# Reordering one time step of two coupled recurrences (a gated recurrent layer and a leaky gated layer) on four engines

## What is computed

```python
# layer 0
z = sigmoid(x_t @ W_z + h @ U_z + cond @ C_z + b_z)
r = sigmoid(x_t @ W_r + h @ U_r + cond @ C_r + b_r)
hh = tanh(x_t @ W + (r * h) @ U + cond @ C + b)
h = (1 - z) * h + z * hh            # x1_t = x_t + h
# layer 1, on x1
gate = sigmoid(h1 @ Wh.T + x1_t @ Wz.T + b)
h1 = tanh(h1 * (1 - alpha) + gate * x1_t)   # x2_t = x1_t + h1
# layers 2 and 3: a scan with forget and input gates, then low-rank adapted dense layers
```

## Time and profile before

| | us |
|---|---|
| median of 3 runs (986.84 to 991.89) | 990.21 |
| the profiled execution | 990.85 |
| its span | 989.0 |
| PE busy | 943.0 (95%) |
| DVE busy | 802.5 (81%) |
| ACT busy | 647.3 (65%) |
| POOL busy | 221.2 (22%) |

### The profile page before, as it was taken

How to read it: one execution, slowest core, us unless ns; L and a number is a source line. 1 busy time by engine, 2 the same in 40 slices (tenths; PEclk the granted TensorE clock), 3 DMA queues, 4 the chain that set the end, 5 groups by cost and what they waited for, 6 DMA issues and landing times.

```text
span 989.0 us, 112546 instructions
## 1 busy us (share of the span) xinstructions
PE 943.0 (95%) x50966; PEld 766.4 (77%) x50966; DVE 802.5 (81%) x2372; ACT 647.3 (65%) x2862; POOL 221.2 (22%) x430
## 2 busy tenths in 40 slices
PE   6699999999999999999999999969999999999996
PEld 5699999999999999999999998335555555555554
DVE  2378778878788778777878787799999999999992
ACT  2478777777777777777777776336455556555552
POOL 0011111111111111111111111324434334434340
PEclk7699999999999999999999999979999999999998
DMA  6113312310010100100101001100011000001001
GB/s 218 41 55 112 110 50 95 111 35 27 24 37 24 37 24 27 34 27 24 37 24 37 24 27 33 28 1 25 24 37 34 24 24 24 24 31 41 24 24 43
DMA packets 38294, 42.01 MB, mean 42 GB/s; under 512 B 5120, under 2 KB 31232, under 8 KB 37120
## 3 DMA queue, kind: packets, MB, share of 16 engines
q1 hardware_dynamic: 36832, 40.55, 13.2%
q10 hardware_dynamic: 1440, 1.18, 0.4%
HBM read 32.80 MB, written 8.91 MB: 42 GB/s over the span
## 4 chain that ended last, share of the span: by engine, by line
PE 57%; DVE 29%; issue 7%; ACT 4%; DMA 1%; ACTq 1%; POOL 0%; DVEq 0%; POOLq 0%
PE bank L788 30%; PE bank L734 22%; DVE arena L667 10%; DVE early L686 4%; DVE early L677 4%; ACT cand_kept L391 2%; DVE early L690 2%; DVE early L684 2%; DVE early L671 2%; DVE early L665 2%; DVE none_h L604 2%; PE bank L906 2%; PE bank L923 1%; DMA bias<-in_bias 1%; PE bank L877 1%
## 5 line engine op out<-in xcount | busy, mean ns | idle before, releaser
L734 PE MATMUL bank<-x_ahead,early 128*32 128x64 f32 x12376 | 345.7, 224 | 5.9 <-ACT bank L358 3.2
L734 PEld LDWEIGHTS bank<-x_ahead,early 128*32 128x32 f32 x12376 | 239.7, 111 | 3.3 <-issue 3.3
L788 PE MATMUL bank<-none_h,early 128*32 128x32 f32 x16384 | 203.1, 199 | 8.8 <-issue 4.9
L280 POOL TENSOR_TENSOR x<-x_f,h_gx 128x64 f32 x256 | 87.6, 342 | 529.4 <-PE bank L788 528.3
L788 PEld LDWEIGHTS bank<-none_h,early 128*32 128x32 f32 x16384 | 180.6, 110 | 27.4 <-DVE none_h L604 13.5
L906 PE MATMUL bank<-x,wl 128*128 (+1 forms) x384 | 182.3, 614 | 0.9 <-DVE rank_rows L646 0.9
L788 PE MATMUL bank<-rh_f,early 128*32 128x32 f32 x8192 | 151.0, 199 | 5.0 <-DVE rh_f L592 2.2
L906 PEld LDWEIGHTS bank<-x,wl 128*128 128x128 f32 x384 | 69.2, 192 | 89.0 <-issue 89.0
L788 PEld LDWEIGHTS bank<-rh_f,early 128*32 128x32 f32 x8192 | 122.1, 112 | 7.0 <-DVE rh_f L592 5.0
L604 DVE TENSOR_TENSOR_SCAN none_h<-zero_z,cand_kept 128x64 f32<-128x64 f32 x512 | 121.6, 279 | 5.3 <-ACT cand_kept L391 3.9
L402 ACT ACTIVATE h_gx<-h_pre 128x64 f32<-128x64 f32 x256 | 68.7, 268 | 81.0 <-DVE h_pre L630 81.0
(11 more groups left out here) (95 smaller groups left out, 1294.4 us busy)
## 6 DMA issues: line engine op xcount, KB each, us to landing
x_in<-in_x SPq DMA_DIRECT2D x34, 256.0 KB, 2.7
x_ahead<-in_x SPq DMA_DIRECT2D x130, 64.0 KB, 1.8
arena<-in_w SPq DMA_DIRECT2D x8, 1024.0 KB, 5.6
out<-y SPq DMA_DIRECT2D x32, 256.0 KB, 2.5
rank_rows<-in_bias_rows SPq DMA_DIRECT2D x1, 1024.0 KB, 5.0
arena<-scratch SPq DMA_DIRECT2D x64, 16.0 KB
early<-in_cx SPq DMA_DIRECT2D x1, 768.0 KB, 4.5
early<-in_wx SPq DMA_DIRECT2D x1, 768.0 KB, 6.3
```

The costliest lines, as they stand in the source:

```text
L280: pool.tensor_tensor(x2[:, :, :, s], x1_f[:, u % LOOP], h1_gx[:, u % 2, :, :, 0], ALU.add).then_inc(x2_done, 1)
L734: mm = pe.matmul(out[32 * j:32 * j + 32], weights(k, j, m), moving(k), start=False, stop=False, tile_position=(0, 32 * j), skip_group_chec ...
L788: mm = pe.matmul(out[32 * j:32 * j + 32], weights(k, j, m), moving(k), start=False, stop=k == 1, tile_position=(0, 32 * j), skip_group_che ...
```

## The change

Instructions of a step are put in another order on PE, ACT and DVE, one is left out, and some waits change. keep_f and its sigmoid go; cand_kept gets (z - 1) h, made by one scalar_tensor_tensor on DVE from zero_z, the tanh is taken of the negated input, and the state scan subtracts instead of adding. On PE both first reset quarters come first, z's mostly behind the reset halves; 32 wide loads, U, layer 1's gate, 32 wide loads follow. "hole" and `late_keep` go. On ACT layer 1's tanh stands behind the reset sigmoids and belongs to one step earlier; its gate comes behind the candidate's tanh, and the reset seeds wait for it. On DVE gate * x1 and the sum of layer 1 come first in a step, x1 of the step before stands behind r * h. r_done and cand_done are counted down by PE, so DVE waits on constants. POOL waits on z_done instead of gate_pre, and its last 16 steps stand behind its loop. SP issues the second x_in load of a turn after the chunk c == 3 of the next one. At the end there is one step of layer 1 more to finish.

```diff
-            def next_turn(n, others=()):
+            def next_turn(n, others=(), first=False):
...
+                    if c == 3 and not first:
+                        next_steps(n - 1, 1)
                     if c == 6:
                         next_steps(n, 0)
...
-                next_steps(n, 1)
@@ POOL
-                    pool.wait_ge(gate_pre, s + LAG + 2)
+                    if last and u >= BODY - LAG - 1:
+                        pool.wait_ge(gate_pre, s + LAG + 2)
+                    else:
+                        pool.wait_ge(z_done, s + LAG + 2)
@@ ACT
-                act.activation(keep_f[:], pre_z[par][:, :, v, :], ACT.Sigmoid, scale=-1.0).then_inc(z_done, 1)
...
-                                   ACT.Tanh).then_inc(cand_done, 1)
+                                   ACT.Tanh, scale=-1.0).then_inc(cand_done, 1)
...
+                    t = n * BODY + u
+                    reset_gate(n, u)
+                    if not first or u > LAG:
+                        second_state(n, u)
+                    elif u:
+                        act.activation(idle[:, u:u + 1], var_eps[:], ACT.Copy).then_inc(h1_done, 1)
+                    update_gate(n, u)
+                    if u % STEPS == 0 and (u or not first):
+                        if first and u <= LAG + 1:
+                            act.wait_ge(gate_pre, u - 1)
+                        else:
+                            act.wait_ge(gate_done, t - LAG - 1)
+                        seed_gate(((u - STEPS) // STEPS) % 2)
+                    candidate(n, u)
+                    if not first or u >= LAG:
                         second_gate(n, u)
...
                     if u % STEPS:
...
+                            act.wait_ge(gate_done, t - LAG + 1)
+                        seed_reset((u // STEPS) % 2, reset_seeded)
                     else:
...
                         seed_keep(1 - (u // STEPS) % 2)
@@ DVE
+            def kept_state(n, u):
+                t, now = n * BODY + u, (u + 1) % 2
+                dve.wait_ge(z_done, t + 1)
+                dve.scalar_tensor_tensor(cand_kept[:, u % 2, :, :, 1], zero_z[:, u % 2, :, :, 1], 1.0,
+                                         none_h[:, now, :, :, 1], ALU.subtract, ALU.mult).then_inc(kept_done, 1)
...
                 for m in range(HALVES):
-                    dve.wait_ge(cand_done, 2 * t + m + 2)
+                    dve.wait_ge(cand_done, m + 1)
                     if m == 0:
-                        dve.wait_ge(kept_done, 2 * t + 2)
+                        dve.wait_ge(kept_done, t + 1)
                     dve.tensor_tensor_scan(pairs(none_h, m), pairs(zero_z, m), pairs(cand_kept, m),
-                                           0.0, ALU.mult, ALU.add).then_inc(h_done, 1)
+                                           0.0, ALU.mult, ALU.subtract).then_inc(h_done, 1)
...
-                    reset_state(n, u)
-                    if second:
+                    if not first or u > LAG:
                         second_gated(n, u)
+                        second_sum(n, u)
+                    reset_state(u)
+                    if u:
+                        first_output(n, u - 1, first)
+                    elif not first:
+                        first_output(n - 1, BODY - 1)
+                    kept_state(n, u)
                     next_state(n, u)
-                    if second:
-                        second_sum(n, u)
-                    first_output(n, u, first)
@@ PE, first_gates
                 pe.wait_ge(h_done, 1)
                 reset(0, 0)
-                keep(0, 0)
-                keep(0, 1)
+                pe.wait_ge(cand_done, 2)
+                reset(0, 1)
+                update(0, 0)
                 pe.wait_ge(h_done, 2)
-                reset(1, 0, taken=h_done).then_inc(r_pre, 1)
-                reset(0, 1)
+                reset(1, 0, taken=(h_done, cand_done)).then_inc(r_pre, 1)
                 reset(1, 1).then_inc(r_pre, 1)
-                keep(1, 0)
-                mm = keep(1, 1)
-                if late_keep:
-                    mm = late_keep()
-                mm.then_inc(z_pre, 1)
+                update(0, 1)
+                update(1, 0)
+                update(1, 1).then_inc(z_pre, 1)
@@ PE, turn
+                for u in range(LOOP):
+                    later = 1 - u // STEPS
+                    first_gates(u)
+                    if u % STEPS == 0:
+                        pe.wait_ge(ahead_loaded[later], 16)
+                        pe.wait_ge(reset_seeded, 2)
+                        ahead_first(later, 0, 0)
+                        ahead_first(later, 0, 1).then_inc(reset_seeded, -2)
+                    else:
+                        ahead_second((u - LAG) % LOOP, later)
+                    first_cand(u)
+                    second_gate(u)
+                    if u % STEPS == 0:
+                        ahead_first(later, 2, 0)
+                        ahead_first(later, 2, 1)
+                    else:
+                        ahead_first(later, 1, 0)
+                        ahead_first(later, 1, 1).then_inc(ahead_loaded[later], -16)
```

More of the change, by code:

```diff
@@ L93, in build_program @@
         rstd = sb("rstd", [P, 1])
-        idle = sb("idle", [P, 2 * LAG])
+        idle = sb("idle", [P, LAG + 1])
         normed = sb("normed", [P, SLAB])
@@ L219, in next_turn @@
                         sp.dma_start(dst, src).then_inc(done, 16)
-                next_steps(n, 1)
-            next_turn(0, [(dst[:], io[name], tail_in) for dst, name in TAIL_LOADS])
+            next_turn(0, [(dst[:], io[name], tail_in) for dst, name in TAIL_LOADS], first=True)
             for w in range(4):
@@ L405, in turn @@
                 for u in range(BODY):
-                    second = not first or u >= LAG
-                    gates_first(n, u)
-                    if second:
+                    t = n * BODY + u
[13 more added lines that the diff above has]
+                    if not first or u >= LAG:
                         second_gate(n, u)
-                    candidate(n, u)
-                    t = n * BODY + u
                     if u % STEPS:
-                        seed_reset((u // STEPS) % 2, 2 * t + 2)
-                    else:
-                        if second or u:
-                            act.wait_ge(z_done, 2 * t)
+                        if first and u < LAG:
+                            act.activation(idle[:, 0:1], var_eps[:], ACT.Copy).then_inc(idle_done, 1)
+                            act.wait_ge(idle_done, 1)
+                        else:
+                            act.wait_ge(gate_done, t - LAG + 1)
+                        seed_reset((u // STEPS) % 2, reset_seeded)
+                    else:
+                        if u or not first:
+                            act.wait_ge(z_done, t)
                         seed_keep(1 - (u // STEPS) % 2)
-                        if second:
[L419 to L426, removed]
                     if first and u == LAG:
@@ L612, in first_output @@
                     dve.wait_ge(x2_done, t - LOOP + 2)
[L613 to L616, removed]
-                    dve.wait_ge(scanned, u + 1)
                 dve.tensor_tensor(x1_f[:, u % LOOP], x_in[:, slot, u % SLOT], none_h[:, nxt, :, :, 1],
@@ L728, in recur, with ahead @@
                 return mm
-            def ahead(out, m, weights, moving, parts=range(HALVES)):
-                for k in parts:
+            def ahead(out, m, weights, moving):
+                for k in range(HALVES):
                     for j in range(SLABS):
@@ L736, in ahead, with ahead_first @@
                 return mm
-            def ahead_first(par, gate, m, parts=range(HALVES)):
+            def ahead_first(par, gate, m):
                 out = (pre_rh[par][m][:, 0], pre_z[par][:, m], pre_rh[par][m][:, 1])[gate]
@@ L772, in _ @@
             pe.wait_ge(seeded, 3)
-            for gate, m in ((0, 0), (0, 1), (2, 0), (2, 1)):
-                ahead_first(0, gate, m)
-            ahead_first(0, 1, 0)
-            ahead_first(0, 1, 1, (0,)).then_inc(ahead_loaded[0], -16)
+            for gate, m in ((0, 0), (0, 1), (1, 0), (1, 1), (2, 0), (2, 1)):
+                mm = ahead_first(0, gate, m)
+            mm.then_inc(ahead_loaded[0], -16)
             pe.wait_ge(hidden_in, 16 * len(HIDDEN_LOADS))
@@ L784, in _, with quarter @@
             pe.wait_ge(weights_in, 16 * len(WEIGHT_LOADS + SECOND_LOADS))
-            def quarter(out, weights, moving, k, m, taken=None):
+            def quarter(out, weights, moving, k, m, taken=()):
                 for j in range(SLABS):
@@ L789, in quarter, with first_gates @@
                                    tile_position=(0, 32 * j), skip_group_check=True)
-                    if taken and j == 1:
-                        mm.then_inc(taken, -2)
+                    if 0 < j <= len(taken):
+                        mm.then_inc(taken[j - 1], -2)
                 return mm
-            def first_gates(u, late_keep=None):
+            def first_gates(u):
```

124 lines of the change are left out of this document (49 added, 75 removed).

## The result

The changed kernel takes 996.85 us (median of 6 runs, 995.75 to 998.37), the kernel before, run beside it, 989.73: ratio 1.0077, 95% interval 1.0057 to 1.0097. The forecast was 974 us, faster; it is slower by 0.8%. Its profiled execution took 996.87 us with a span of 995.0.

What follows compares the result with a forecast made beforehand. 249 steps of 2.252 us, with 0.23 of PE gaps from one chain, bound the kernel. Four steps, 2.10 + 2.10 + 2.16 + 2.37 = 8.73 against 9.01, save 17.3 us, less 1.0 = 16.3: 974 us (966 to 982, chance 0.50).

Steps and rivals of the forecast that it cites:

- (6): DVE: second layer's product and sum before the reset product, ending at 0.76 to 0.78 where 0.79 is wanted; taken as 0.
- (7): DVE: kept state from z alone in one instruction, usable by 1.54 to 1.70, before the scan at 1.76; costs nothing.
- (4): PE loop's back edge: 0.31 us nearly uncovered, fourth step 2.37; ACT's and DVE's 0.25 every 16 steps goes.
- (8, 9): SP's x loads: zero, at most 0.3 us in one step of 16; POOL waking on z: zero.
- step (3): Chain of a new step: first reset sigmoid 0.56, tanh 1.53, scan 1.76, next step 2.10; PE ends at 2.07.
- (5): ACT's reset seeds, awaited by PE's wide products: 0 to 0.07 us in one step of four, 0.06 taken, 2.16.
- PE's work, 2.02: PE's loads in one step: 0.58 state products, 0.26 gate, 0.28 U, 64 wide at 0.014; unchanged by the change.
- Rival D: PE stalls more than counted (seeds, small loads at 9.3 ns, two waits): +0.05 a step, 12 us, 986; chance 0.15.
- Rival C: PE's back edge hides behind queued work: 17 us more gain, 957; chance 0.15 together with other gains below 966.
- (10): Loop's end: one more product, sum and tanh of the second layer open, plus 1.0 us (0.5 to 2).
- start-up: Before the loop: same instructions, 0 +- 2 us.

Runs made afterwards that it cites:

- a_spread: Changed kernel with PE's count-downs of cand_done and r_done moved off matmuls next to other semaphore updates: 993.42 us, 1.0050 of the kernel before.
- a_swap: Changed kernel with the two waits before the wide reset products exchanged, seeds first, then x chunk: 994.26 us, 1.0060 of the kernel before.
- a_quiet: Changed kernel with the count-downs of h_done and cand_done moved from reset(1, 0) to reset(1, 1): 995.87 us, 1.0092 of the kernel before.
- b_free: Kernel before with four unused semaphore updates added on one wide quarter in steps 0 and 2 of each turn: 987.36 us, 1.0003.

## Why the prediction was wrong

Right: in the steps, the second layer's order on DVE (6) and kept (7) cost nothing; ACT's and DVE's back edge every 16 steps is gone (4); SP and POOL (8, 9) show nothing; the chain is a little shorter than before (2.13 to 2.17 with PE relieved, where the first three steps of before take 2.165, 2.21 and 2.23). The direction fell on three terms, each too small, in the sum of step (3) to (5): 8.73 forecast, 9.16 measured a turn.

**PE's work, 2.02, and with it step (3)**: +0.175 a turn (2.19 + 2.185 for twice 2.10). "Instruction counts on PE stay the same: 2.02 us a step" took the gate's 0.24 to 0.26 from a run that stands behind a wait, where its 32 loads go at 7.5 ns. Dense behind U they take 0.37 to 0.39: 0.272 at the dense pace and some 0.10 for four updates. Before, wide loads stood 32 places behind U, and its updates cost nothing; with the gate there they do. Part of it could be read in the trace of before, in the step of the earlier trace rows, where the gate has no wait in front of it and takes 0.41 - 0.11 = 0.30:

```profile
306.78 0.41 PEld L788 LDWEIGHTS bank<-h_gx,early 128*32 128x32 f32 x32
```

The state products take 0.64 for 0.58. The 0.58 is what they take behind a wait, which the kernel before had in front of two steps of four; in the other two they take 0.61 to 0.62. Behind a wait the first 32 need 0.25, in the dense run 0.31. The rest is the new update for cand_done, 0.026 by a_spread. The change took away the waits that had hidden all this. Rival D had the direction of this ("small loads at 9.3 ns"), but 0.05 a step as its price for everything, 986 us. The chain was 0.07 too short besides, so that even a PE with little to do would have given 2.13 to 2.17.

**The back edge (4)**: 2.50 for 2.37, +0.13. The mechanism was right, 0.32 uncovered where 0.31 was taken. But it comes behind a PE that ends at 2.18, not at 2.07: the same missing PE work once more, which accounts for 0.11 of it. Before, the back edge made the fourth step 0.13 longer than the second, which has the same work (2.34 against 2.21); now it is 0.32. Rival C is wrong: nothing hides.

**The seeds (5)**: 2.281 for 2.16, +0.12. The ordinary step's 0.085 is in it, and 0.035 is the second wait behind the seeds (a_swap). The seeds end at +0.61 for 0.56, since the gate ends later, and the wide products start at +0.73, outside the bound of 0.61 to 0.70. With the waits exchanged the seeds' step is still 0.06 longer than the ordinary one, as the prediction took it.

The drain (10) was -2.0 instead of +1.0, start-up -1.4: a gain of 4.4 against the forecast that covers part of the loss; where it comes from wasn't looked into, so that much of the time is luck. Per turn 0.43, times 62.25, is 26.8; less 4.4 is 22.4, and 974.6 + 22.4 = 997.0, the time of the profiled execution.

No version of the changed kernel that does all the work beats the kernel before. The nearest, with seeds waited for first and the updates moved (989.8), is 0.3% behind. Its steps are 2.162, 2.180, 2.206 and 2.504, against 2.229, 2.208, 2.230 and 2.342 before (means, the back edges of ACT and DVE in them): 0.12 gained in three, 0.16 lost in the fourth.

## What to carry to other kernels

When a change takes the idle time out of the bound engine, price its work by rows from dense stretches and not by runs that stand behind a wait, and ask which fixed costs (a loop's back edge, semaphore updates, a second wait) lay over that idle time. A chain that is made shorter than the engine's dense work gains nothing beyond it. On a kernel like this one, look through the new order for dense small loads that stand 32 places behind a matmul that updates a semaphore, and put updates where wide loads stand at that distance, but not right in front of the matmul that another engine waits for.

## What the hardware showed that was not expected

- A semaphore update on a matmul costs 0.025 us of the weight loads 32 places later if these are small and dense (four added: +0.10 in U, 1003.9 us). It costs nothing if they load for 64-column products (a_quiet, that run at 0.420 us) or stand right behind such loads (b_free, 1.0003).
- 32 small loads take 0.24 to 0.25 us behind a wait and go at 17 ns for two in a dense run, 0.272 for 32 without updates; right behind wide loads they take 0.31.
- A PE loop of four steps (1536 loads and matmuls) leaves 0.20 MB of instructions fetched in all; one of eight steps (3072) fetches 6.90 MB, and the kernel takes 1.95 times as long.
- A PE back edge makes its step 0.10 to 0.13 us longer behind idle time and 0.31 to 0.36 behind work. Why it varies from 0.31 to 0.36 between kernels of equal length stays open, as does why an update acts 32 loads later.
